# Four-layer graph network on one core: halved relu, mask add and norm steps in the second layer, a DVE copy in the first, two-input DVE forms throughout

## The reference

```python
h = jnp.maximum(_layernorm(x, axis=-1), 0.0)
x = x + _L0_gnn_ref(h, adj, ...)   # dot-product attention, 1 head
h = jnp.maximum(_layernorm(x, axis=-1), 0.0)
x = x + _L1_gnn_ref(h, adj, ...)   # 4 heads, leaky_relu of the scores
h = jnp.maximum(_layernorm(x, axis=-1), 0.0)
x = x + _L2_gnn_ref(h, adj, ...)   # additive attention over 64 features, elu
h = jnp.maximum(_layernorm(x, axis=-1), 0.0)
x = x + _L3_gnn_ref(h, adj, ...)   # src + dst scores, residual, elu, layer norm with gamma, beta
```

## Time and profile before

| what | value |
|---|---|
| median of 3 runs | 3586.21 us (3578.19 to 3587.32) |
| profiled execution, own time | 3591.9 us |
| its span, first to last instruction | 3590.1 us |
| mean granted TensorE clock | 0.956 |
| busy PE, PEld, DVE, ACT, POOL | 86%, 47%, 85%, 81%, 28% |
| layer 0, layer 1, layer 2, layer 3 | about 28 to 262, 305 to 1272, 1297 to 3222, 3236 to 3590 us |

### The profile page before, as it was taken

The page is one execution under the profiler, slowest core; times in us unless marked ns, Lnnn a source line. Parts: engine busy times, 40 slices in busy tenths (PEclk is TensorE's granted clock), DMA queues, the critical chain, the costliest instruction groups (busy, mean ns, idle before and its releaser), DMA issues. The chain is left out here.

```text
span 3590.1 us, 77844 instructions
## 1 busy us (share of the span) xinstructions
PE 3095.4 (86%) x30972; PEld 1700.4 (47%) x30972; DVE 3037.3 (85%) x4709; ACT 2911.2 (81%) x3505; POOL 1018.2 (28%) x629
## 2 busy tenths in 40 slices
PE   7987998999999969888898898888988988978886
PEld 5664666666666633333333333333333333336665
DVE  6666787778777779999999999999999999975665
ACT  4665777777777759999999999999999999975665
POOL 4433665556656600000000100000001010005764
PEclk9998999999999979999999999999999999987777
DMA  7630000000000000000000000000000000002211
GB/s 244 213 132 20 21 21 21 19 19 21 20 19 21 18 10 10 10 10 10 7 13 10 10 10 10 10 10 7 13 10 10 10 7 13 10 5 69 57 56 33
DMA packets 68394, 111.44 MB, mean 31 GB/s; under 512 B 26452, under 2 KB 26582, under 8 KB 68054
## 3 DMA queue, kind: packets, MB, share of 16 engines
q1 hardware_dynamic: 68054, 106.69, 9.7%
HBM read 86.61 MB, written 18.87 MB: 29 GB/s over the span
## 5 line engine op out<-in xcount | busy, mean ns | idle before, releaser
L1029 ACT ACTIVATE l_scalar_ring<-l_w,l_r 128x1024 f32<-128x1024 f32 x1632 | 1713.1, 1142 | 37.9 <-DVE l_values L1075 27.6
L1143 DVE TENSOR_SCALAR l_vector_ring<-l_w_code,l_r_code 128x2048 f32<-128x2048 f32 x1232 | 1588.9, 1354 | 3.5 <-issue 0.6
L966 PE MATMUL scores<-l_scalar_ring,l_signs 128*32 128x512 f32 x6528 | 794.1, 605 | 90.7 <-ACT l_scalar_ring L1029 90.4
L976 PE MATMUL scores<-l_vector_ring,l_signs_code 128*32 128x512 f16 x9856 | 673.3, 395 | 136.7 <-DVE l_vector_ring L1143 135.8
L242 ACT COPY probs_t<-turned 128x512 f32<-128x512 f32 x576 | 324.3, 586 | 484.9 <-PE turned L201 484.8
L450 POOL TENSOR_TENSOR l_masked<-l_relu,mask 128x1024 f32<-128x1024 f32 x256 | 545.7, 2132 | 419.8 <-ACT l_relu L607 384.6
L976 PEld LDWEIGHTS scores<-l_vector_ring,l_signs_code 128*32 128x32 bf16 x9856 | 243.3, 96 | 589.8 <-DVE l_vector_ring L1143 300.8
L201 PE MATMUL turned<-ident,l_probs 128*128 128x128 f32 x3072 | 440.6, 289 | 12.1 <-issue 7.9
L269 ACT ACTIVATE l_probs<-l_logits,negmax 128x1024 f32<-128x1024 f32 x384 | 443.5, 1155 | 7.6 <-DVE negmax L260 7.6
L966 PEld LDWEIGHTS scores<-l_scalar_ring,l_signs 128*32 128x32 f32 x6528 | 201.0, 110 | 469.6 <-issue 262.9
L260 DVE CUSTOM_DVE_ANT_0 l_logits<-scores,l_masked,l_bound 128x1024 f32<-128x1024 f32 x256 | 328.3, 1282 | 107.3 <-POOL l_masked L450 73.1
(11 more groups left out here) (240 smaller groups left out, 3129.4 us busy)
## 6 DMA issues: line engine op xcount, KB each, us to landing
mask<-masks_kept SPq DMA_DIRECT2D x192, 256.0 KB, 2.6
l_adj<-adj SPq DMA_DIRECT2D x64, 512.0 KB, 5.7
masks_kept<-l_mask_ring SPq DMA_DIRECT2D x64, 256.0 KB, 4.7
x_res<-x SPq DMA_DIRECT2D x8, 256.0 KB, 5.1
out<-x_res SPq DMA_DIRECT2D x8, 256.0 KB, 2.7
l_h<-l_h SPq DMA_DIRECT2D x8, 128.0 KB, 2.9
l_kl<-l_dh SPq DMA_DIRECT2D x32, 2.0 KB, 1.8
l_kl<-l_dl SPq DMA_DIRECT2D x32, 2.0 KB, 1.8
```

The source lines that it names most:

```text
L966: last = nc.tensor.matmul(s.scores[g * ROWS:(g + 1) * ROWS, buf, half, :], signs[:, window], scalar_ring[:, at % SCALAR_RING, g, halves[ha ...
L976: last = nc.tensor.matmul(s.scores[g * ROWS:(g + 1) * ROWS, buf, half, :], signs_code[:, par, g % 2, window], parts(vector_ring[:, at % VE ...
L1029: last = nc.scalar.activation(scalar_ring[:, at % SCALAR_RING, g, :], w[:, par, :], ACT.Relu, bias=r[:, par, column:column + 1])
L1143: last = nc.vector.tensor_scalar(vector_ring[:, at % VECTOR_RING, g:g + 2, :], w_code[:, par, :, :], r_code[:, par, 0, column:column + 1], ...
```

## The change

Six edits:

1. Layer 1, relu and mask: ACT's relu is issued as two halves of 512 columns, each released by its own half of the scores (PE signals each half). POOL adds the mask in two halves, the first as soon as the first half of the relu is there.
2. Layer 1, norm: DVE's mean sum is halved over units 0 and 2, POOL's centring over 4 and 6, its square over 8 and 10, DVE's variance sum over 12 and 14; the root stands at unit 16, the product is halved over 18 and 20, and the values move from unit 6 to unit 22.
3. Layer 0: DVE takes the first half of the copy of the turned probabilities; ACT keeps the second.
4. All layers: the scaling of mean and variance (`mean_of`, `variance`) becomes a `scalar_tensor_tensor` whose second input is a constant tile of zeros or of the epsilon.
5. Layers 0, 1 and 3: the values are taken by a `scalar_tensor_tensor` with `y` as both inputs.
6. Layer 3: both ELU parts become `scalar_tensor_tensor` with the same tile as both inputs. The minimum comes first and releases `elu_parts` alone; the -1 moves into the later sum, which gets a `drain` ahead of it.

```diff
+def mean_of(s, stat):
+    return s.nc.vector.scalar_tensor_tensor(out=stat[:, 1, :], in0=stat[:, 0, :], scalar=1.0 / s.D, in1=s.zeros[:], op0=ALU.mult,
+                                            op1=ALU.add)
...
-    return s.nc.vector.tensor_scalar(stat[:, 3, :], total, 1.0 / s.D, LN_EPS, ALU.mult, ALU.add)
+    return s.nc.vector.scalar_tensor_tensor(out=stat[:, 3, :], in0=total, scalar=1.0 / s.D, in1=s.eps[:], op0=ALU.mult, op1=ALU.add)
...
-                g.wait_ge(sems["relu_ready"], u + 1)
+                g.wait_ge(sems["relu_ready"], 2 * u + 1)
                 wait(g, sems["logits_ready"], STARTS + u - 1)
-                nc.gpsimd.tensor_tensor(masked[:, n % 2, :], relu4[:, n % 2, :], s.mask[:, i, :], ALU.add
-                                        ).then_inc(sems["masked_ready"], 1)
+                for half in range(2):
+                    cols = slice(half * BANK, (half + 1) * BANK)
+                    if half:
+                        g.wait_ge(sems["relu_ready"], 2 * u + 2)
+                    last = nc.gpsimd.tensor_tensor(masked[:, n % 2, cols], relu4[:, n % 2, cols], s.mask[:, i, cols], ALU.add)
+                last.then_inc(sems["masked_ready"], 1)
...
+                    if leaky and n in (4, 6):
+                        centre_half(next_norm(s, b), b + 2, n // 6)
+                    if leaky and n in (8, 10):
+                        square_half(b + 2, n // 10)
+                    if leaky and n == 16:
+                        root(b + 2)
+                    if leaky and n in (18, 20):
+                        apply_half(par, b + 2, b + 1, n // 20)
...
-                    last = nc.tensor.matmul(out, h1[:, par, rows], kl[:, par, h, cols], start=False, stop=True)
-                last.then_inc(sems["scores_ready"], 1)
+                    nc.tensor.matmul(out, h1[:, par, rows], kl[:, par, h, cols], start=False, stop=True).then_inc(sems["scores_ready"], 1)
...
             def relu(n, u):
-                a.wait_ge(sems["scores_ready"], u + 1)
                 wait(a, sems["masked_ready"], u - 1)
-                nc.scalar.activation(relu4[:, n % 2, :], scores[n % 2], ACT.Relu, scale=1.0 / SLOPE - 1.0
-                                     ).then_inc(sems["relu_ready"], 1)
+                for half in range(2):
+                    a.wait_ge(sems["scores_ready"], 2 * u + half + 1)
+                    nc.scalar.activation(relu4[:, n % 2, half * BANK:(half + 1) * BANK], s.scores[:, n % 2, half, :], ACT.Relu,
+                                         scale=1.0 / SLOPE - 1.0).then_inc(sems["relu_ready"], 1)
...
-                    if not leaky:
-                        copy_half(a, nc.scalar.copy, s, sems, 0, u)
...
-                    if leaky:
-                        copy_half(v, nc.vector.tensor_copy, s, sems, 0, u)
+                    copy_half(v, nc.vector.tensor_copy, s, sems, 0, u)
...
+                    if leaky and n in (0, 2):
+                        mean_half(next_norm(s, b), b + 2, n // 2)
+                    if leaky and n in (12, 14):
+                        scale_half(b + 2, n // 14)
...
-                    if n == (6 if leaky else 4) and project:
+                    if n == (22 if leaky else 4) and project:
                         take_values(b + 1, 1 - par)
...
-                elu_parts(v, s, sems, z[:, par, :, :], low, high)
+                out = z[:, par, :, :]
+                nc.vector.scalar_tensor_tensor(out=low[:], in0=out, scalar=0.0, in1=out, op0=ALU.min, op1=ALU.min
+                                               ).then_inc(sems["elu_parts"], 1)
+                nc.vector.scalar_tensor_tensor(out=high[:], in0=out, scalar=0.0, in1=out, op0=ALU.max, op1=ALU.max)
```

More of the change, by code:

```diff
@@ new lines, in mask_relu, with centre_half @@
+                last.then_inc(sems["masked_ready"], 1)
+            def centre_half(b, done, half):
+                if half == 0:
+                    g.wait_ge(sems["mean_ready"], done + 1)
+                    wait(g, sems["y_ready"], done)
+                rows = slice(half * NB // 2, (half + 1) * NB // 2)
+                last = nc.gpsimd.tensor_tensor(s.centred[:, rows, :], s.graph(b)[:, rows, :],
+                                               s.stat[:, 1, rows].unsqueeze(2).to_broadcast([P, NB // 2, D]), ALU.subtract)
+                if half:
+                    last.then_inc(sems["centred_ready"], 1)
@@ new lines, in square_half, with root @@
+            def square_half(done, half):
+                if half == 0:
+                    g.wait_ge(sems["centred_ready"], done + 1)
+                rows = slice(half * NB // 2, (half + 1) * NB // 2)
+                last = nc.gpsimd.tensor_tensor(s.square[:, rows, :], s.centred[:, rows, :], s.centred[:, rows, :], ALU.mult)
+                if half:
+                    last.then_inc(sems["square_ready"], 1)
+            def root(done):
+                g.wait_ge(sems["seed_ready"], done + 1)
+                inverse_root(g, s, s.stat, s.stat[:, 7, :])
@@ new lines, in apply_half @@
+            def apply_half(par, done, taken, half):
+                if half == 0:
+                    g.drain()
+                    g.wait_ge(sems["values_ready"], taken)
+                    wait(g, sems["fill_ready"], (taken - 1) * K + 2)
+                rows = slice(half * NB // 2, (half + 1) * NB // 2)
+                last = nc.gpsimd.tensor_tensor(s.y[:, par, rows, :], s.centred[:, rows, :],
+                                               s.stat[:, 7, rows].unsqueeze(2).to_broadcast([P, NB // 2, D]), ALU.mult)
+                if half:
+                    last.then_inc(sems["y_ready"], 1)
@@ L674, in logit, with mean_half, scale_half @@
                                mask_ring[:, n % SLOTS, :])
+            def mean_half(b, done, half):
+                if half == 0:
+                    wait(v, sems["y_ready"], done)
+                rows = slice(half * NB // 2, (half + 1) * NB // 2)
+                nc.vector.tensor_reduce(s.stat[:, 0, rows], s.graph(b)[:, rows, :], AX.X, ALU.add)
+                if half:
+                    v.drain()
+                    mean_of(s, s.stat).then_inc(sems["mean_ready"], 1)
+            def scale_half(done, half):
+                if half == 0:
+                    v.wait_ge(sems["square_ready"], done + 1)
+                rows = slice(half * NB // 2, (half + 1) * NB // 2)
+                nc.vector.tensor_reduce(s.stat[:, 2, rows], s.square[:, rows, :], AX.X, ALU.add)
+                if half:
+                    v.drain()
+                    variance(v, s, s.stat, s.stat[:, 2, :]).then_inc(sems["seed_ready"], 1)
             def inverse_sum(n):
@@ L1556, in out_mean @@
             def out_mean(b):
+                v.drain()
                 v.wait_ge(sems["elu_exp"], b + 1)
-                nc.vector.tensor_tensor(work[:, 2, :, :], high[:], low[:], ALU.add)
+                nc.vector.scalar_tensor_tensor(out=work[:, 2, :, :], in0=high[:], scalar=-1.0, in1=low[:], op0=ALU.add, op1=ALU.add)
                 v.drain()
```

28 lines of the change are left out of this document (16 added, 12 removed).

## The result

The changed kernel takes **3532.93 us** (median of 4 runs, 3528.05 to 3536.67) where the kernel before took 3586.77 beside it (3578.19 to 3591.84). The ratio is 0.9849 with a 95% interval from 0.983 to 0.9869, so 53.8 us are gone; 42.3 were forecast. The profiled executions have spans of 3590.1 and 3534.6 us.

The account below looks back on a forecast made before the run. PE, fullest in layers 0 and 1, was taken as held by waits, layer 1 by its relu-to-scores chain; layer 2 keeps its time. Terms -20 -6.5 -3 -4.8 +4 -10 -2 = -42.3 from 3586.2 gave 3544 us, range 3516 to 3574.

Parts of the forecast that it names:

- Layer 1's sum: Layer 1: relu and mask -20 us, mean -6.5, square -3, variance -4.8, values +4, root and product nothing.
- the chain's term: Layer 1: relu, mask add, L260, output copy, L234, scores set the pace; halves shorten it, 20 us gained.
- Copy in layer 0: Layer 0: PE's 13.5 us wait for ACT's copy goes, DVE's added copy costs 3.5; net -10 us.
- Relu and mask in halves: Layer 1: path 0.29 us shorter, passed once in three units, pace 3.34 to 3.25; -20 us (0 to 25).
- Mean, square, variance: Layer 1 norm: halved steps shorten PE's stalls at units 0, 4 and after 8; -6.5, -3 and -4.8 us.
- values: Layer 1, unit 22: two-input form and wait for a half add delay the next probabilities copy; +4 us (0 to 8).
- Root and product: Layer 1: costed at nothing; POOL's wait for the relu covers the product, otherwise about 0.5 us lost per graph.
- ACT pays 0.06 per unit: Layer 1: two half relus cost ACT 0.06 us more per unit, 15 us in all, beside PE's work.
- Layer 3, -2: Layer 3: ACT's exponential waits for the first ELU part alone, but both parts get 0.26 longer; -2 us (-8 to +5).
- The slower one: Rival, chance 0.10: layer 1's half adds take above 1.28 us and lengthen the path; 3621 us at 1.607.
- the limit of layer 1: Rival, chance 0.22: DVE becomes the limit, the 20 us from halved relu and mask do not come; 3564 us.
- The two-input form: Rival: scalar_tensor_tensor is free of POOL, another 10 to 16 us gone, about 3530; chance 0.13 shared with everything coming.

Follow-up runs that it names:

- e3: Changed kernel with ACT again taking both halves of layer 0's copy of the turned probabilities: 3545.24 us, layer 0 at 231.9 us.
- e11: Changed kernel with layer 1's mean and variance scalings on ACT, and its relu and mask add whole again: 3538.10 us, layer 1 at 929.8 us.
- e8: Changed kernel with layer 1's scalings of mean and variance moved from DVE to ACT: 3524.05 us, layer 1 at 919.9 us.
- e1: Changed kernel with layer 1's relu and mask add whole again, the rest kept: 3569.41 us, layer 1 at 955.3 us.
- e2: Changed kernel with layer 1's norm steps whole and at their old units, values at unit 6, relu and add still halved: 3539.53 us, layer 1 at 939.8 us.
- e6: Changed kernel with three unused PE products per unit added in layer 3: 3562.27 us, layer 3 at 327.9 us.
- e7: Kernel before the change with three unused PE products per unit added in layer 3: 3592.99 us, layer 3 at 326.5 us.
- e4: Changed kernel with layer 3's old ELU instructions and sum put back: 3550.77 us, layer 3 at 323.9 us.
- e12: Kernel before the change with only layer 1's scalings of mean and variance moved to ACT: 3570.72 us, layer 1 at 939.7 us.

## Why the prediction was right, and where it was not

The time came out at 3532.9, in the range and at the fast edge of what the forecast itself had (3532 to 3557). Layer 0 was right for the reason given. Layer 1's sum, 30.4 against 30.3, is luck: the chain's term was 10 us too large, the root's 8 too small, a hold worth 17 stood in no term as a gain, and the errors cancel. Layer 3 was not right.

*Copy in layer 0, -10.* Right to the tenth in the stretches, and e3 gives it back whole.

*Relu and mask in halves, -20.* Here the step that failed is "It is passed once in three units, so the pace goes from 3.34 to 3.25". The path relu to add did shorten, by the 0.28 forecast as 0.29 (median 3.22 before, 2.94 after), but it sets the time only in some units. Its worth is 9.9 us (e11 against e8), half of my term. Taken out alone the edit was worth 27.3, because it also cut the hold of the mean's scaling (2.02 in e1, 0.70 in the changed kernel), 17.4. I had that effect in the next term ("held as the old one was, but by a half add"), and there it was sized as a remaining wait and not as a gain of this edit. The 18.6 of e2 lie near my 20 by chance. The 3.34 was itself read off three units; the distances 18 to 31 are 3.49 on average before and 3.46 after.

*Mean, square, variance, -14.3, and values, +4.* Together -10.3; undone (e2) they cost 11.8 and made alone (e1) they gave 3.1. The 11.8 are no proof of the 10.3: 7.4 of them lie at distance 15 (4.04 in e2, 3.11), which is the root and product's, and leave 4.4. By place: the square's distance 6 gave 0.48 a graph (3.8 us, I had 3). The values cost about 1 us where I had 4: the distances 22 to 25 sum to 14.29 in e2 and 14.42 in the changed kernel. The mean's stall went as described but was larger (distance 2 fell from 5.79 to 3.85, 15.5 us where I had 10.5), and its new scaling costs 0.76 a graph at distance 4 (4.70 against e8's 3.94) where I had 0.5.

*Root and product, 0.* Wrong. I saw POOL's wait for the relu as cover, and there was more to win: distance 15, three units behind the old root and product, fell from 4.10 to 3.11, which is 8 us, and is 4.04 in e2. (The list of POOL's order with the change ends two units behind the root; the two halves of the product, L497, 0.62 each, come next, with two units' adds between them.) In return distance 16 rose by 0.92 and 17 fell by 0.50. The scaling of the variance on DVE is not the whole of it: with it on ACT (e8) the distances 16 to 18 sum to 11.35, against 11.39 with it and 11.03 before. What costs the 0.3 us a graph there, the half sum, the root or the product, is not tested.

*ACT pays 0.06 per unit.* Right: its busy time in layer 1 rose from 725.6 to 739.0, 13 us, where I had 15. By the rule of the Trainium skill (VectorE: DVE Perf Modes, The TRN2 errata) it would have been, as an estimate, 37. In the trace a half relu takes 0.59 and two in a row end after 1.07, so that part of the one lies under the other.

*Layer 3, -2.* At nearly equal clocks the ELU edit gave between 5 us and a loss (e6 and e7), so the 2 us for its path are neither shown nor refuted. What failed is that I took the stretch of 0.78 clock as a constant. It isn't: the clock moved the stretch between 295 and 324 us, and layer 3's 14.7 us instead of 2 are more than the 11.5 by which the forecast missed. That the ELU edit itself has a part in the better clock is likely, since by the medians neither kernel with the old ELU gained more than 1 us there (e4, e12), but the way is open.

*The rivals.* The slower one's condition did not come: the half adds stayed at 1.16, below 1.28. DVE did not become the limit of layer 1; it still waited 42.8 us for the masked relu. The two-input form was not free: its scaling lasted up to 1.12 us. No run undoes the two-input forms of the scalings and the values by themselves, so what they cost or give against the old forms is not shown.

## What to carry to other kernels

Look for the smallest instruction that ends at the same moment as a large one of POOL; moved to ACT, where each took some 0.3, two such scalings of 0.17 us on DVE gave 18.7 us of 958, more than a reorganisation of the whole norm alone (3.1). Cutting a long chain shortens only the units in which its last step is what is waited for: average the unit distances by place, before and after, and not only the waits. Two edits that relieve the same hold must be tested both ways round, since each looks worth 9 us more when undone than when made alone.

## What the runs showed of the hardware that was not expected

The granted clock of layer 3 differs between kernels whose code there is the same (0.80 to 0.90, 315 to 295 us), though an edit upstream is all that separates them; in one place it fell to 0.50 behind PE waits of 1.5 to 1.9 us, while added PE work went with 0.93 in one case and with 0.84 in another. DVE's sums with one input were never held: 0.40 us in each of 16, 14 of them beside one of POOL's half adds, where its scalings lasted up to 1.12 beside half adds and 2.08 beside whole ones:

```profile
L744 DVE TENSOR_REDUCE stat<-x_res x16: 398/399/401, 304.0 to 1127.9; 128x4 f32 x12, 128x4 f32<-128x256 f32 x4
L136 DVE SCALAR_TENSOR_TENSOR stat<-stat,zeros x8: 1121/2018/2083, 312.8 to 1155.9; 128x8 f32<-128x8 f32 x8
```

(the first of e8, the second of e1). And POOL's root on 128x8 takes 1.65 us, more than a subtraction on 128x256, 0.62.
